# SwiGLU gates moved ahead of the second product, sixteen expert outputs summed in one PSUM bank, the token sort moved to the front of each mixture, and GpSimd in the GELU mixtures left with data movement alone

## The chip, the cores and the metric

One core of one Trainium2 chip runs the kernel. The metric is device time in microseconds (us) of one execution; the figure given is the median of three runs. The core's engines run side by side, each through its own list of instructions in order, and wait for each other on semaphores: PE (TensorE, matrix products), ACT (ScalarE), DVE (VectorE), POOL (GpSimd) and SP (SyncE, which here only issues DMAs).

## The reference

The network has four layers; each is a convolution-like mixer and then a mixture of experts over 8192 tokens of 64 channels, with a layer norm ahead of both. Layers 0 and 3 have a SwiGLU mixture of 16 experts of hidden size 128, layers 1 and 2 a GELU mixture of 8 experts of hidden size 256; each token uses the two experts with the largest router logits. Cut to the two mixtures:

```python
# SwiGLU, layers 0 and 3
h1 = jnp.einsum('bsd,edh->bseh', x, w1)
h2 = jnp.einsum('bsd,edh->bseh', x, w2)
hidden = jax.nn.silu(h1) * h2
expert_out = jnp.einsum('bseh,eho->bseo', hidden, w3)
return jnp.einsum('bseo,bse->bso', expert_out, dispatch)   # dispatch: two non-zero gates per token
# GELU, layers 1 and 2
for e in range(E):
    h = jax.nn.gelu(xf @ W1[e] + b1[e], approximate=False)
    out = out + w_dense[:, e:e + 1] * (h @ W2[e] + b2[e])
```

The third product is linear, so a SwiGLU gate may multiply the output of an expert or its hidden activations. In the GELU mixture the bias b2 stands between the product and the gate.

## The kernel before, in words

The tokens lie as 8 chunks of 512 columns, two halves of 64 channels stacked on the 128 partitions. In each mixture the first 6 chunks are *dense*: every expert is computed for every token and the gates (zeros among them) pick. A *step* is one expert on one chunk: 96 steps in SwiGLU, 48 in GELU; a *round* is two steps. The last 2 chunks (the pair SORTED) are *sorted*: DVE computes for each of their tokens a place in a list ordered by expert, POOL scatters the tokens to that list in DRAM (32 indirect DMAs, L757), the list is loaded (L792), worked off expert by expert in a *phase* on all engines (L824 to L924: 16 turns in SwiGLU, 12 in GELU, each with its own weights fetched by SP, L778 and L780), stored (L806), and POOL gathers two results for each token (32 indirect DMAs, L765), which are weighed (L942), merged on PE (L950) and added (L958). The phase interrupts the dense steps ahead of step `AFTER` (60 of 96, 30 of 48).

A SwiGLU step has three layers. PE forms the first (L1013, three products of split numbers); ACT applies Silu to both halves (L1167); PE forms the second, and DVE multiplies it in (L1187). Of an even step DVE multiplies both halves (128x1024), of an odd step one half; ACT copies the other half out of PSUM (L1157, `mx_kept`), and POOL multiplies it (L1268). PE forms the third layer into one of two small banks (L1099); DVE multiplies the result by the gates (L1194, `mx_gated`), and the product is added into `x` (L559): by POOL, or in the rounds in which POOL scatters or gathers (`by_vector`) by DVE. The gates are transposed by PE, written to DRAM (L539) and spread back over partitions by SP (L550, two DMAs of 128 KB a step, a ring of four slots).

A GELU step has two blocks of 128 hidden units: PE L1013, ACT Gelu L1401, PE L1350 into one of two small banks, DVE L1422 (bias and gate in one instruction), and the add (L559), again on POOL outside of the rounds with moves. POOL's list for GELU is: four conversions of tokens (L485), adds of steps 0 to 14, 32 scatters, 5 adds, 32 gathers, 5 adds.

The top-two choice is 17 small DVE instructions per pair of chunks (`choose`, L423 to L447; one Tanh on ACT, L455, lies ahead of the 13th), the sort 24 (`sort`, L691 to L746, with two count products on PE, L673). Before, both are handed out over the rounds of the first chunks (`between`, `behind`), the SORTED pair first. SP's one list serves all: spreads of gates, weights, the loads of sorted tokens (`load_at`, waiting for all scatters) and the stores. DVE's list, POOL's list and SP's list are written out by hand; nothing reorders them.

## Time and profile before

| | us |
|---|---|
| median of three runs (least, most) | 1908.18 (1907.76, 1908.95) |
| profiled execution | 1910.55 |
| its span in the trace | 1908.8 |
| busy PE, DVE, ACT, POOL in the span | 1630.5, 1163.1, 913.6, 780.2 |
| SwiGLU of layer 0, of layer 3 (first Silu to last add) | 350.7, 351.7 |
| GELU of layer 1, of layer 2 | 229.2, 232.3 |

Matmuls overlap in the records, so PE's busy time in a full stretch is near its length. "granted clock" is the share of TensorE's full 2.4 GHz that was granted; 0.50 is the lower of its two levels. The four mixtures take 1164 us of the 1908.8; the mixers and norms between them are not touched.

### The profile page before, as it was taken

How to read it: one execution, taken by the hardware profiler on the slowest of the kernel's cores; microseconds unless marked ns; L12 is line 12 of the kernel's file. 1: busy time of each engine (PE TensorE's matmuls, PEld its weight loads, DVE VectorE, ACT ScalarE, POOL GpSimd, SP SyncE). 2: the span in 40 equal slices, each digit the busy share in tenths (PEclk: the TensorE clock that was granted, in tenths of full speed). 3: DMA queues.
4: the chain of work that ended last, by engine and by line, in shares of the span. 5: the costliest groups of instructions: out<-in, count | busy, mean ns of one | idle time of the engine just before them, and what ended most of it. 6: DMA issues, size and time to landing. Idle time of an engine off the chain costs nothing. (4 is left out here: it accounts for less than half of the span.)

```text
span 1908.8 us, 32576 instructions
## 1 busy us (share of the span) xinstructions
PE 1630.5 (85%) x11943; PEld 928.0 (49%) x11943; DVE 1163.1 (61%) x1716; ACT 913.6 (48%) x1499; POOL 780.2 (41%) x711
## 2 busy tenths in 40 slices
PE   6878889789689979898978997999999678888787
PEld 3644444444244434444434445777777344444444
DVE  6678885387865512465631346665666478885386
ACT  2444444444236646435546544666666344434343
POOL 3316673176023623412360626333332036673275
PEclk8989999999799989999989998999999789999899
DMA  6012235242203443301253330000000012344233
GB/s 163 1 38 79 93 114 141 85 112 82 88 4 74 105 123 89 77 21 38 67 154 94 82 93 1 2 1 2 2 1 1 3 49 87 93 124 140 85 110 101
DMA packets 96922, 134.46 MB, mean 70 GB/s; under 512 B 31316, under 2 KB 48660, under 8 KB 96116
## 3 DMA queue, kind: packets, MB, share of 16 engines
q1 hardware_dynamic: 88564, 123.88, 22.9%
q0 software_dynamic: 8192, 8.40, 1.9%
q8 instruction: 99, 1.62, 0.4%
q14 instruction: 67, 0.55, 0.1%
HBM read 115.30 MB, written 16.91 MB: 69 GB/s over the span
## 5 line engine op out<-in xcount | busy, mean ns | idle before, releaser
L1013 PE MATMUL ps<-tokens_high,w_high 64*128 64x512 f32 x1152 | 259.8, 446 | 64.4 <-DVE mx_hidden L1187 56.3
L559 POOL TENSOR_TENSOR x<-x,mx_gated 128x512 f32<-128x512 f32 x144 | 188.7, 1311 | 285.7 <-DVE mx_gated L1422 218.5
L2458 DVE TENSOR_TENSOR c_near_weights<-c_near_hats 128x768 f32<-128x768 f32 x192 | 189.9, 1036 | 103.1 <-PE ps L2329 103.0
L1401 ACT ACTIVATE mx_hidden<-ps,w_bias 128x1024 f32<-128x1024 f32 x192 | 198.3, 1115 | 97.8 <-PE ps L1013 97.8
L1187 DVE TENSOR_TENSOR mx_hidden<-ps,mx_hidden 128x1024 f32<-128x1024 f32 x192 | 184.0, 958 | 88.3 <-PE ps L1013 86.9
L1013 PE MATMUL ps<-tokens_low,w_high 64*128 64x512 f32 x1152 | 234.0, 401 | 0.0
L1013 PE MATMUL ps<-tokens_high,w_low 64*128 64x512 f32 x1152 | 233.4, 400 | 0.0
L1268 POOL TENSOR_TENSOR mx_hidden<-mx_kept,mx_hidden 128x512 f32<-128x512 f32 x94 | 130.6, 1390 | 228.7 <-ACT mx_kept L1157 228.2
L1013 PEld LDWEIGHTS ps<-tokens_high,w_high 64*128 64x128 f32 x1152 | 111.8, 189 | 213.9 <-DVE mx_hidden L1187 133.3
L1350 PE MATMUL ps<-mx_hidden,w_second 128*64 128x512 f32 x768 | 184.4, 618 | 32.7 <-DVE mx_gated L1422 25.5
L1099 PE MATMUL ps<-mx_hidden,w_second 128*64 128x512 f32 x768 | 194.6, 624 | 9.4 <-DVE mx_gated L1194 6.6
L1422 DVE SCALAR_TENSOR_TENSOR mx_gated<-ps,w_bias,mx_gates 128x512 f32<-128x512 f32 x96 | 72.0, 750 | 213.8 <-PE ps L1350 146.6
L1167 ACT ACTIVATE mx_hidden<-ps 128x1024 f32<-128x1024 f32 x192 | 187.3, 1022 | 17.6 <-PE ps L1013 7.5
L1157 ACT COPY mx_kept<-ps 128x512 f32<-128x512 f32 x94 | 55.1, 587 | 276.1 <-PE ps L1013 270.0
L2407 ACT COPY c_near_matrix<-ps 128x512 f32<-128x512 f32 x288 | 149.0, 608 | 8.2 <-PE ps L2329 7.3
L757 POOL DMA_INDIRECT sorted_board<-mx_by_laid,mx_by_rows x128 | 128.8, 1006 | 42.5 <-issue 42.1
L2436 POOL TENSOR_TENSOR c_near_dist<-c_near_position,c_ints 128x288 f32<-128x288 f32 x64 | 65.1, 1017 | 193.8 <-DVE c_near_hats L2448 191.0
L765 POOL DMA_INDIRECT mx_by_tokens<-out_board,mx_by_rows x128 | 128.0, 1000 | 35.3 <-issue 33.4
L1194 DVE TENSOR_TENSOR mx_gated<-ps,mx_gates 128x512 f32<-128x512 f32 x192 | 127.9, 683 | 21.8 <-PE ps L1099 13.9
L2329 PE MATMUL ps<-identity,c_near_weights 128*128 128x128 f32 x1152 | 138.4, 277 | 0.0
L2358 PE MATMUL ps<-c_near_matrix,c_near_values 128*64 128x128 f32 (+1 forms) x1536 | 135.4, 329 | 0.0
L2329 PEld LDWEIGHTS ps<-identity,c_near_weights 128*128 128x128 f32 x1152 | 126.7, 142 | 11.4 <-issue 10.1
(275 smaller groups left out, 2416.1 us busy)
## 6 DMA issues: line engine op xcount, KB each, us to landing
mx_gates<-gate_board SPq DMA_DIRECT2D x576, 128.0 KB
mx_by_tokens<-sorted_board SPq DMA_DIRECT2D x14, 512.0 KB, 5.3
out_board<-mx_by_tokens SPq DMA_DIRECT2D x14, 512.0 KB, 2.8
w_first<-in_f_first SPq DMA_DIRECT2D x4, 1024.0 KB, 11.8
mx_by_first<-in_f_first_of SPq DMA_DIRECT2D x64, 64.0 KB
mx_by_second<-in_f_second_of SPq DMA_DIRECT2D x48, 65.0 KB
mx_by_first<-in_f_first_of SPq DMA_DIRECT2D x48, 64.2 KB
c_weight<-in_c_weight SPq DMA_DIRECT2D x1, 2304.0 KB
```

The source lines that it names most:

```text
L559: engine.tensor_tensor(place, place, gated, ALU.add).then_inc(self.s.added.semaphore, 1)
L1013: last = pe.matmul(out[h], weights[w][half(h), w_own], tokens[t][half(h), t_own], start=(p == 0), stop=(p == 2))
L1099: last = pe.matmul(out.bank("step", n)[half(h), :], w.second[:, e * C:(e + 1) * C], hidden[:, n % HIDDEN, h, :], start=True, stop=True)
L1167: act.activation(hidden[:, n % HIDDEN], first[:, n % FIRST], ACT.Silu).then_inc(s.act.semaphore, 1)
L1187: dve.tensor_tensor(own, second[:, 0:halves, :], own, ALU.mult).then_inc(s.hidden.semaphore, 1)
L1268: pool.tensor_tensor(own, kept[:, m // 2 % KEPT, :], own, ALU.mult).then_inc(s.other.semaphore, 1)
L1350: last = pe.matmul(out.bank("step", n)[half(h), :], w.second[:, (e * F + f) * C:(e * F + f + 1) * C], hidden[:, n % HIDDEN, f, h, :], star ...
L1401: act.activation(hidden[:, n % HIDDEN, f], first[:, (n * F + f) % BLOCKS], ACT.Gelu, bias=w.bias1[:, e * F + f:e * F + f + 1]).then_inc(s. ...
L2329: last = pe.transpose(turned[:, c % BANKS, at:at + P], weights[:, (HALVES * n + h) % SLOTS, t, q * P:(q + 1) * P], k.identity[:])
L2358: last = pe.matmul(acc[half(h), ty // (QTILES // 2), to:to + count * P], values[:, (v // G) % RING, g, h, t * C:(t + 1) * C], matrix[:, h, ...
L2407: act.copy(own, turned[:, c % BANKS, :].rearrange("p (h b c) -> p h b c", h=HALVES, c=P)).then_inc(s.matrix, 1)
L2458: dve.tensor_tensor(weights[:, u % SLOTS].rearrange("p t (r c) -> p t r c", c=W), spread(own[:, :, W:W + ROWS], 3, W), spread(own[:, :, 0: ...
```

## The change

SwiGLU:

- The gates multiply the hidden activations of a step after Silu and ahead of the second product: DVE those of half 0, POOL those of half 1 (both 128x512, both operands in SBUF). The spread gates now hold both halves on all partitions: one DMA of 512 KB a step in place of two of 128 KB.
- The third layers of a chunk's 16 experts accumulate in one PSUM bank (bank 6); DVE adds it into `x` once per chunk: 6 adds in place of 96. L1194 goes. The other small uses share bank 7.
- The multiply of the kept half moves from POOL (L1268) to DVE (`multiply_kept`).
- PE forms first layers one step further ahead.
- Scatters start at step 6 and gathers at step 50, two per round in place of three. The phase stands ahead of step 48 instead of 60.

Both mixtures:

- The choice of the SORTED pair (11 of its instructions) and the whole sort stand on DVE ahead of the first step; PE's count products stand in the first round.
- Loads and stores of the sorted tokens are issued by POOL and not by SP.

GELU:

- All 48 adds are on DVE. POOL's list is four conversions, 32 scatters, 3 loads, 3 stores, 32 gathers.
- The phase stands ahead of step 24 instead of 30. In it, the copies of columns and of outputs (with bias) move from ACT to DVE.

The core of the diff:

```diff
@@ class Gates, prefetch of step n
+        if self.of_hidden:
+            if n >= self.SLOTS:
+                self.s.gated_other.wait(sp, n - self.SLOTS + 1)
+            rows = self.board.rearrange("(h e) c -> e h c", h=HALVES)[e, :, chunk(i)]
+            sp.dma_start(self.spread[:, n % self.SLOTS, :, :], rows.partition_broadcast(P)).then_inc(
+                self.s.gate[n % self.SLOTS].semaphore, 16)
+            return
@@ class ByExpert
-    def load(self, sp):
+    def load(self, pool):
-    def store(self, sp, g):
-        self.s.turned.wait(sp, (g + 1) * (self.GROUP // 4))
-        sp.dma_start(self.group(self.out_board, g), self.own_group(g)).then_inc(self.s.stored.semaphore, 16)
+    def store(self, pool):
+        for g in range(self.m.slots // self.GROUP):
+            self.s.turned.wait(pool, (g + 1) * (self.GROUP // 4))
+            pool.dma_start(self.group(self.out_board, g), self.own_group(g)).then_inc(self.s.stored.semaphore, 16)
@@ mixture_swiglu, tensor
+            if e == 0 and i >= 1:
+                s.added.wait(pe, i)
             for h in range(HALVES):
-                last = pe.matmul(out.bank("step", n)[half(h), :], w.second[:, e * C:(e + 1) * C],
-                                 hidden[:, n % HIDDEN, h, :], start=True, stop=True)
+                last = pe.matmul(sums[half(h), :], w.second[:, e * C:(e + 1) * C],
+                                 hidden[:, n % HIDDEN, h, :], start=(e == 0), stop=(e == E - 1))
...
+            if n == 0:
+                gates.turn(pe, 0, small.bank("gates", 0))
+                for c in range(2):
+                    small.free(pe, "count", c)
+                    by.count_up(pe, c, small.bank("count", c))
             second_layer(n)
@@ mixture_swiglu, vector
+            s.gated.wait(dve, n + 1)
+            s.gated_other.wait(dve, n + 1)
             halves = HALVES if n % 2 == 0 or n == STEPS - 1 else 1
             own = hidden[:, n % HIDDEN, 0:halves, :]
             dve.tensor_tensor(own, second[:, 0:halves, :], own, ALU.mult).then_inc(s.hidden.semaphore, 1)
...
         def gate(n):
-            s.third.wait(dve, n + 1)
+            s.act.wait(dve, n + 1)
             gates.wait(dve, n)
...
+            own = hidden[:, n % HIDDEN, 0, :]
+            dve.tensor_tensor(own, own, gates.spread[:, n % gates.SLOTS, 0, :], ALU.mult).then_inc(s.gated.semaphore, 1)
...
         choose(0, 12, 17)
+        choose(SORTED, 0, 11)
+        sort(0, by.OPS)
+        gate(0)
         for n in range(0, STEPS, 2):
             if n >= 2 and n != AFTER:
                 multiply(n - 1)
-            between(n // 2)
+                multiply_kept(n - 1)
+            if n >= E + 2 and n % E == 2 and n - 2 != AFTER:
+                add(n // E - 1)
+            between(n)
+            gate(n + 1)
             multiply(n)
...
+            if n + 2 < STEPS:
+                gate(n + 2)
@@ mixture_swiglu, gpsimd
+            gate(n + 1)
+            if n == AFTER - 2:
+                by.store(pool)
+            if n + 2 < STEPS:
+                gate(n + 2)
...
+            if n == SCATTER_AT + 2 * (MOVES // EACH) + 2:
+                by.load(pool)
@@ mixture_gelu, vector
-            if by_vector(n):
-                gates.add(dve, n, gated[:, n % GATED, :])
+            gates.add(dve, n, gated[:, n % GATED, :])
...
         choose(0, 12, 17)
+        choose(SORTED, 0, 11)
+        sort(0, by.OPS)
@@ mixture_gelu, gpsimd
+        for i in range(2 * by.NT):
+            by.scatter(pool, i)
+        by.load(pool)
+        by.store(pool)
+        for i in range(2 * by.NT):
+            by.gather(pool, i)
```

In what follows each row is an instruction, a run of like ones with its count behind "x"; names are as in the text above, `gt_` those of the choice, `ln_square` and `mx_by_` those of the sort. DVE at the start of the first SwiGLU mixture before, from the last instruction of the first pair's choice (L447) on:

```order
L447 TENSOR_TENSOR gate<-gt_equal,gt_rank 128x256
L423 TENSOR_REDUCE gt_best<-gt_logits 128x16
L425 TENSOR_TENSOR gt_equal<-gt_logits,gt_best 128x256
L427 TENSOR_TENSOR gt_rank<-gt_equal,countdown 128x256
L1187 TENSOR_TENSOR mx_hidden<-ps,mx_hidden 128x1024
L1187 TENSOR_TENSOR mx_hidden<-ps,mx_hidden 128x512
```

The same place now (the first and the last rows of the 37 that stand between L444, which was L447, and the first multiply):

```order
L444 TENSOR_TENSOR gate<-gt_equal,gt_rank 128x256
L420 TENSOR_REDUCE gt_best<-gt_logits 128x16
L422 TENSOR_TENSOR gt_equal<-gt_logits,gt_best 128x256
...
L749 TENSOR_REDUCE mx_by_number<-mx_by_passed 1x32
L751 TENSOR_SCALAR mx_by_expert<-mx_by_number 1x32
L1222 TENSOR_TENSOR mx_hidden<-mx_hidden,mx_gates 128x512
L420 TENSOR_REDUCE gt_best<-gt_logits 128x16
L422 TENSOR_TENSOR gt_equal<-gt_logits,gt_best 128x256
L1222 TENSOR_TENSOR mx_hidden<-mx_hidden,mx_gates 128x512
L1211 TENSOR_TENSOR mx_hidden<-ps,mx_hidden 128x1024
```

Three instructions of the sorted pair stood ahead of the first multiply; now its whole choice but for the last part, the sort, two gates and two instructions of the next pair do. POOL in the rounds with scatters of SwiGLU before, a round to every two rows:

```order
L757 DMA sorted_board<-mx_by_laid,mx_by_rows 8192x64 x3
L1268 TENSOR_TENSOR mx_hidden<-mx_kept,mx_hidden 128x512
L757 DMA sorted_board<-mx_by_laid,mx_by_rows 8192x64 x3
L1268 TENSOR_TENSOR mx_hidden<-mx_kept,mx_hidden 128x512
L757 DMA sorted_board<-mx_by_laid,mx_by_rows 8192x64 x3
```

And now, with the loads behind the last scatters:

```order
L1287 TENSOR_TENSOR mx_hidden<-mx_hidden,mx_gates 128x512 x2
L762 DMA sorted_board<-mx_by_laid,mx_by_rows 8192x64 x2
L1287 TENSOR_TENSOR mx_hidden<-mx_hidden,mx_gates 128x512 x2
L762 DMA sorted_board<-mx_by_laid,mx_by_rows 8192x64 x2
L1287 TENSOR_TENSOR mx_hidden<-mx_hidden,mx_gates 128x512 x4
L797 DMA mx_by_tokens<-sorted_board 128x1024 x4
L1287 TENSOR_TENSOR mx_hidden<-mx_hidden,mx_gates 128x512 x5
L802 DMA out_board<-mx_by_tokens 128x1024 x4
```

A round held one tensor instruction and three moves on POOL; it holds two and two. POOL in a GELU mixture, whole, before:

```order
L485 TENSOR_TENSOR tokens_low<-xn,tokens_high 128x512 x4
L559 TENSOR_TENSOR x<-x,mx_gated 128x512 x15
L757 DMA sorted_board<-mx_by_laid,mx_by_rows 6144x64 x32
L559 TENSOR_TENSOR x<-x,mx_gated 128x512 x5
L765 DMA mx_by_tokens<-out_board,mx_by_rows 128x64 x32
L559 TENSOR_TENSOR x<-x,mx_gated 128x512 x5
```

And now:

```order
L482 TENSOR_TENSOR tokens_low<-xn,tokens_high 128x512 x4
L762 DMA sorted_board<-mx_by_laid,mx_by_rows 6144x64 x32
L797 DMA mx_by_tokens<-sorted_board 128x1024 x3
L802 DMA out_board<-mx_by_tokens 128x1024 x3
L770 DMA mx_by_tokens<-out_board,mx_by_rows 128x64 x32
```

The scatters no longer stand behind adds, and the loads stand right behind them on the same queue.

## Rows read from the trace of the kernel before

**Rows 1.** Table by stretch: length, busy us by engine, clock, DMA share, GB/s.
```profile
126.30:477.00 350.70, 298.23 (x1872) 157.39 (x1876) 255.34 (x358) 148.58 (x208) 196.80 (x163) 0.97 0.36 101
570.80:800.00 229.20, 203.10 (x1256) 100.09 (x1258) 90.48 (x165) 130.17 (x182) 99.54 (x92) 0.96 0.37 94
678.30:692.00 13.70, 5.29 (x22) 1.18 (x20) 1.49 (x2) 0.27 (x1) 3.50 (x3) 0.50 0.76 211
```
**Rows 2.** Waits of PE in layer 0's SwiGLU: total us, times, longest.
```profile
PE ps L1013 <- DVE mx_hidden L1187: 28.3, 30, 4.3
```
**Rows 3.** Timeline of ACT: start, us, instruction, [idle before <-releaser].
```profile
126.29 1.92 ACT L1167 ACTIVATE mx_hidden<-ps 128x1024 f32<-128x1024 f32 x2
...
233.81 1.94 ACT L1167 ACTIVATE mx_hidden<-ps 128x1024 f32<-128x1024 f32 x2
...
281.82 1.94 ACT L1167 ACTIVATE mx_hidden<-ps 128x1024 f32<-128x1024 f32 x2
293.92 1.94 ACT L1167 ACTIVATE mx_hidden<-ps 128x1024 f32<-128x1024 f32 x2
...
1865.78 0.59 ACT L1157 COPY mx_kept<-ps 128x512 f32<-128x512 f32 x1 [2.98 <-PE ps L1013]
1871.39 0.58 ACT L1157 COPY mx_kept<-ps 128x512 f32<-128x512 f32 x1 [2.96 <-PE ps L1013]
...
1884.11 0.59 ACT L1157 COPY mx_kept<-ps 128x512 f32<-128x512 f32 x1 [4.39 <-PE ps L1013]
1888.97 0.59 ACT L1157 COPY mx_kept<-ps 128x512 f32<-128x512 f32 x1 [2.21 <-PE ps L1013]
```
**Rows 4.** Timeline of POOL, two rounds with gathers.
```profile
1819.10 1.29 POOL L1268 TENSOR_TENSOR mx_hidden<-mx_kept,mx_hidden 128x512 f32<-128x512 f32 x1
...
1821.84 0.94 POOL L765 DMA_INDIRECT mx_by_tokens<-out_board,mx_by_rows  x1 [0.30 <-issue]
1823.09 0.94 POOL L765 DMA_INDIRECT mx_by_tokens<-out_board,mx_by_rows  x1 [0.30 <-issue]
1824.08 1.67 POOL L1268 TENSOR_TENSOR mx_hidden<-mx_kept,mx_hidden 128x512 f32<-128x512 f32 x1
```
**Rows 5.** Timeline of DVE: the same rounds, layer 0's early rounds, GELU's start, the end.
```profile
128.54 0.42 DVE L425 TENSOR_TENSOR gt_equal<-gt_logits,gt_best 128x256 f32<-128x256 f32 x1
129.00 0.42 DVE L427 TENSOR_TENSOR gt_rank<-gt_equal,countdown 128x256 f32<-128x256 f32 x1
129.34 1.22 DVE L1187 TENSOR_TENSOR mx_hidden<-ps,mx_hidden 128x1024 f32<-128x1024 f32 x1
...
134.64 1.39 DVE L433 SCALAR_TENSOR_TENSOR gt_logits<-gt_one_hot,gt_logits 128x256 f32<-128x256 f32 x1
...
582.81 0.29 DVE L427 TENSOR_TENSOR gt_rank<-gt_equal,countdown 128x128 f32<-128x128 f32 x1
...
1823.08 1.53 DVE L559 TENSOR_TENSOR x<-x,mx_gated 128x512 f32<-128x512 f32 x2
...
1902.10 0.69 DVE L559 TENSOR_TENSOR x<-x,mx_gated 128x512 f32<-128x512 f32 x1 [0.27 <-POOL x L559]
```
**Rows 6.** Waits of PE in layer 1's GELU.
```profile
PE ps L1350 <- DVE mx_gated L1422: 12.2, 5, 8.4
PE ps L514 <- DVE gate L447: 1.6, 1, 1.6
```
**Rows 7.** Timeline of PE around the phase's start in layer 1's GELU.
```profile
677.27 2.74 PE L1350 MATMUL ps<-mx_hidden,w_second 128*64 128x512 f32 x8 [2.41 <-DVE mx_gated L1422]
...
688.98 5.09 PE L1350 MATMUL ps<-mx_hidden,w_second 128*64 128x512 f32 x16 [8.41 <-DVE mx_gated L1422]
```
**Rows 8.** Timeline of SP's queue there.
```profile
680.62 1.29 SPq L792 DMA_DIRECT2D mx_by_tokens<-sorted_board  x3
```
**Rows 9.** Timeline of POOL: the last scatter there, and GELU's start.
```profile
572.41 4.99 POOL L485 TENSOR_TENSOR tokens_low<-xn,tokens_high 128x512 fp32r<-128x512 f32 x4 [11.47 <-DVE gate L447]
...
678.47 0.96 POOL L757 DMA_INDIRECT sorted_board<-mx_by_laid,mx_by_rows  x1 [0.30 <-issue]
```

More of the change, by code:

```diff
@@ L401, in __init__ @@
         self.pairs = k.mixtures * self.PAIRS
-        dense = m.dense // 2
-        order = [0] + list(range(dense, self.PAIRS)) + list(range(1, dense))
-        self.turn_of = {pair: i for i, pair in enumerate(order)}
     def done(self, pair):
@@ L587, in store @@
     def store(self, sp, i):
-        self.s.added.wait(sp, self.E * (i + 1))
+        self.s.added.wait(sp, self.adds * (i + 1))
         self.put(sp, i)
@@ L1015, in split_product, with out_order @@
     return last
-def out_order(steps, E, dense, turn_at, lay_at, count_at, after, merge_at):
-    order = [("gates", 0)]
-    for n in range(steps):
-        order.append(("step", n))
-        if n % E == turn_at and n // E + 1 < dense:
-            order.append(("gates", n // E + 1))
+def out_order(uses, dense, turn_at, lay_at, after, merge_at):
+    order = [("gates", 0), ("count", 0), ("count", 1)]
+    for n, own in enumerate(uses):
+        order += own
+        if n in turn_at:
+            order.append(("gates", turn_at.index(n) + 1))
         if n in lay_at:
             order.append(("lay", lay_at.index(n)))
-        if n == count_at:
-            order += [("count", 0), ("count", 1)]
         if n == after - 1:
@@ L1263, in _, with gate @@
     def _(pool):
-        def multiply(m):
-            s.act.wait(pool, m + 1)
-            s.kept.wait(pool, m // 2 + 1)
-            own = hidden[:, m % HIDDEN, 1, :]
-            pool.tensor_tensor(own, kept[:, m // 2 % KEPT, :], own, ALU.mult).then_inc(s.other.semaphore, 1)
-        pool.wait_ge(k.gt.gates, top_two.done(0))
-        for n in range(2, STEPS + 2, 2):
-            if n < STEPS:
-                multiply(n - 1)
-            if n % 4 == 2 and EARLY + n // 4 < DENSE:
-                token_low(k, pool, tokens, EARLY + n // 4)
-            for a in (n - 3, n - 2):
-                if a >= 0 and not by_vector(a):
-                    gates.add(pool, a, gated[:, a % GATED, :])
+        def gate(n):
+            s.act.wait(pool, n + 1)
+            gates.wait(pool, n)
+            own = hidden[:, n % HIDDEN, 1, :]
+            pool.tensor_tensor(own, own, gates.spread[:, n % gates.SLOTS, 1, :], ALU.mult).then_inc(
+                s.gated_other.semaphore, 1)
+        pool.wait_ge(k.gt.gates, top_two.done(0))
+        token_low(k, pool, tokens, EARLY)
+        gate(0)
+        for n in range(0, STEPS, 2):
+            gate(n + 1)
+            if n == AFTER - 2:
+                by.store(pool)
+            if n + 2 < STEPS:
+                gate(n + 2)
+            if 0 <= n - 8 < 2 * (DENSE - EARLY - 1):
+                token_low(k, pool, tokens, EARLY + 1 + (n - 8) // 2)
             for i in range(EACH):
@@ L1359, in second_layer @@
                 by.lay(pe, unit, out.bank("lay", unit))
-            if n == COUNT_AT:
-                for c in range(2):
-                    out.free(pe, "count", c)
-                    by.count_up(pe, c, out.bank("count", c))
             if n in MERGE_AT:
@@ L1373, in _ @@
                 gates.turn(pe, 0, out.bank("gates", 0))
+                for c in range(2):
+                    out.free(pe, "count", c)
+                    by.count_up(pe, c, out.bank("count", c))
             if n >= 2 and n != AFTER:
@@ L1481, in _ @@
             token_low(k, pool, tokens, i)
[L1482 to L1489 removed]
+        pool.wait_ge(k.gt.low, lows(k, DENSE - 1))
+        for i in range(2 * by.NT):
[4 more added lines that the diff above has]
+            by.gather(pool, i)
+        s.added.wait(pool, STEPS)
     @block.sync
```

332 lines of the change are left out of this document (150 added, 182 removed).

## The prediction

> **What bounds the kernel now.** I read the page first: PE is busy 85% of the span, the four mixtures take 1164 us of it, and only these change. Then the table by stretch for each mixture [rows 1]: in 350.70 us of SwiGLU PE is busy for 298.23, in 229.20 us of GELU for 203.10, so what can be won without touching a matmul is about 50 and 25 us a mixture, whoever is made faster. Then PE's waits show for whom it waits: in SwiGLU for DVE's multiply of the hidden activations [rows 2], 28.3 us in 30 pieces; in GELU for DVE's gate, 12.2 us in 5 pieces with one of 8.4 [rows 6].
>
> The starts of ACT's instructions give the length of a round of SwiGLU [rows 3]. A round in which POOL adds takes 4.86 us (1884.11 to 1888.97); ACT waits for PE in it, no round is shorter, and I take this as PE's own pace. A round in which DVE adds because POOL moves tokens takes 5.61 (1865.78 to 1871.39). The first 17 rounds, between which the choice and the sort are spread, take 233.81 - 126.29 = 107.5, against 17 x 4.86 = 82.6. One round takes 12.10 (281.82 to 293.92): SP stands in front of the load of sorted tokens there, and the gates behind it come late.
>
> Last I read single instructions of DVE and POOL side by side. POOL's multiply starts at 1824.08 while two adds of DVE (1823.08, 1.53 long, to 1824.61) run; it takes 1.67, against 1.29 at 1819.10, where no add of DVE runs [rows 4, 5]. On DVE the choice's instruction at 134.64 takes 1.39 while its neighbours of the same kind and size take 0.42 [rows 5]. Both have two operands in SBUF. So DVE and POOL hold each other up there, in both directions; the multiply that reads PSUM (1.22 at 129.34) shows no such spread.
>
> The Trainium skill says the same in "SBUF — State Buffer", section "Who interferes with whom": a DVE instruction with two SBUF inputs and a GpSimd instruction that reads SBUF exclude each other for a whole instruction. The trace agrees (1.67 for 1.29, 1.39 for 0.42). By that rule the change is a bad trade, since it turns DVE work that reads PSUM into work with two SBUF operands; this is my first rival, below, with its price from rows.
>
> **The change, part by part.** The sum is made against the profiled execution, 1910.55 us, which is 2.4 above the median of 1908.18; the difference is then taken off the median.
>
> *SwiGLU, what goes.* (a) The excess of the first 17 rounds: 107.5 - 82.6 = 24.9. (b) The excess of rounds with adds on DVE: 24 of them (steps 30 to 53 and 60 to 83), two already in (a), 22 x 0.75 = 16.5. (c) The load leaves SP's queue, so the round of 12.10 becomes an ordinary one: 6.5. (d) The last add waits for POOL's (0.27 at 1902.10 [rows 5]) and for a gate on DVE of 0.69 ahead of it: about 1. In the phase SP issues no stores between fetches: I take 1. Together 49.9.
>
> *SwiGLU, what comes.* (e) Ahead of the first multiply DVE has 11 instructions of the choice and 24 of the sort. The choice's pitch is 129.00 - 128.54 = 0.46 [rows 5]: 5.1. The sort at the same pitch is 11.0, and it goes through PE twice for the counts, some 1.5. POOL converts one chunk and multiplies its first gates meanwhile; each can hold DVE up as at 134.64, 1.39 - 0.42 = 0.97, so 2 for two of them. Together 19.6. Bounds: 16 (nothing held up, shorter instructions), 24 (every second instruction met by POOL). Nothing hides it: PE has two first layers in hand and then waits. PE at rest is granted the lower clock afterwards: where it rested 10.8 us around 680, the clock was 0.50 for 13.7 us [rows 1, 7]; I take 2 for it, from 0 to 7.
>
> (f) Rounds with moves: 16 for scatters, 16 for gathers. POOL has two multiplies (1.29) and two moves at a pitch of 1823.09 - 1821.84 = 1.25 [rows 4]: 5.08. DVE now has three instructions with two SBUF operands (two of 0.69 for gates or kept half, one more for the other gate), beside 1.22 + 0.69 that read PSUM: 3 x 0.69 + 1.91 = 4.0, so POOL is the longer list. It is held up by DVE as at 1824.08, 0.38. Once per round gives 5.46, so 32 x (5.46 - 4.86) = 19.2. Bounds: never, 32 x 0.22 = 7.0; both multiplies behind a whole instruction of 0.69 each, 5.08 + 1.38 = 6.46, 51.2. I take once, as the rows of a round with moves show one per round.
>
> (g) Choices of pairs 1 and 2 fall in 12 rounds, two instructions each, about one of them with two SBUF operands and so open to POOL: 0.97 x 8 = 7.8, from 0 to 12. (h) Six adds of the sum bank, 0.69 each and the wait of PE for the bank at each chunk: 3, from 0 to 6. (i) One gate DMA of 512 KB for 256 KB a step, and 16 rounds without moves: DVE's 4.0 and POOL's 2.6 lie beneath PE's 4.86, and DMA's mean share of 0.36 [rows 1] leaves room; 0, up to 5 if gates come late. (e) to (h): 19.6 + 2 + 19.2 + 7.8 + 3 = 51.6.
>
> So SwiGLU comes out at +1.7 a mixture, nought within what I can tell, and +3.4 for two. The adds removed (90 of 96) buy nothing by themselves, because rounds with adds on POOL already went at PE's pace.
>
> *GELU, what goes.* (j) PE stands 2.41 and 8.41 us ahead of the phase [rows 7]. SP shows why: the load of sorted tokens leaves it at 680.62, after the last scatter (678.47 + 0.96 [rows 9]), and the gates of the next steps stand behind that load in the same queue [rows 8]. With the load on POOL this goes: 10.8. What could be late next is the load itself, at 24 steps instead of 30: POOL has four conversions in 5 us and 32 scatters at the pitch of 1.25, 45 us together, and the scatters wait for a sort that ends some 14 us in, so they end near 60 us; step 24 of 48 stands at about half of the mixture's 229 less a share for the phase, some 80 to 100. 20 or more are left for the load. (k) The clock of 0.50 for 13.7 us, in which PE was busy for 5.29 [rows 1]: half of it, 2.6. (l) The turn of gates that waits for the choice, 1.6 [rows 6], as the choice is done earlier. (m) The rest of 12.2, where adds on POOL or DVE and choice meet: 1.4. (n) In merges, in the steps around the phase and in its turns small things, 3 together, bounds 0 and 6: moving columns and outputs from ACT to DVE can win only where PE waits for ACT, and none of PE's two large waits is for ACT [rows 6]. Sum 19.4.
>
> *GELU, what comes.* (o) DVE starts the sorted pair's choice when POOL starts its four conversions (572.41, 4.99 us for four [rows 9]). Choice of 11 at 0.29 + 0.04 [rows 5] is 3.6; each conversion holds DVE up once for about 1.0, so 7.6, then the sort's first instruction, and PE's counts come 6.9 later than PE would be free for them. PE stands for it, with 1.5 of lower clock behind: 8.4. Bounds 3 (conversions do not hold DVE up) and 14. The rest of the sort lies beside PE's next first layers and the trip of the first gates through DRAM. (p) All 48 adds on DVE: 0.69 each, 33 us at most on an engine that is busy for 90 of 229 [rows 1]: 0. Sum 8.4, so GELU gains 11.0 a mixture, 22.0 for two.
>
> Total: 3.4 - 22.0 = -18.6, 1908.2 - 18.6 = 1889.6. My bounds of (e) are as wide on the short side as on the long one, those of (f) lean to the long side, (n) and (m) to more gain. I forecast 1890.
>
> **The rivals.**
>
> *DVE and POOL lock each other out (slower).* Place: the 32 rounds with moves of each SwiGLU mixture. If both of POOL's multiplies wait for a whole instruction of DVE, and DVE's instructions wait likewise, a round takes 6.46 and not 5.46: 2 x 32 x 1.0 = +64 at the most; half of it, 5.96 per round, is the likelier form, +32: 1890 + 32 = 1922. It decides from 0.34 us per round on (22 us over 64 rounds, with which 1890 passes 1912). For it: 1.67 and 1.39 [rows 4, 5], and that each round holds five such instructions where it held three. Against it: POOL's moves, half of its round, show no change beside DVE's adds (0.94 throughout), and give DVE time for its own.
>
> *They hardly meet (faster).* PE runs further ahead, so DVE and POOL may fall into a pattern in which DVE's three instructions always lie beside POOL's moves. Then a round takes 5.08, (f) is 7.0 and (g) nought: -20 a mixture, 1890 - 40 = 1850. For it: two moves take 2.5, three DVE instructions 2.07. Against: DVE's order puts a PSUM multiply between them.
>
> *GELU's stall stays.* If scatters, now one string of 32 ahead of a load on the same queue, end late, or DVE's adds make gates late, (j) and (k) stay: 13.4 a mixture, 1890 + 26.8 = 1917; with half of it, 1903. Against: 20 us to spare.
>
> *The start costs more.* If the low clock holds after the opening, at 7 for 2 in SwiGLU and (o) at 14, with (e) at 24: 2 x (5 + 4.4 + 5.6) = +30, 1920. For it: a rest as long as this one is nowhere in these mixtures; against: (a) contains the same instructions, with the same locks.
>
> **How the numbers follow.** A measurement of this kernel can tell 0.2%, 3.8 us, from no change: faster is below 1904.4, slower above 1912. Chances: forecast 0.48 (1872 to 1904 alone), lock-out 0.19, hardly meet 0.14, GELU's stall 0.07, start 0.12. Faster: 0.47 of the forecast, 0.14, and 0.03 of partial cases of the others: 0.64. Slower: 0.15 of the lock-out, 0.03 and 0.07 of the last two: 0.25. Same is left with 0.11. The range leaves out a tenth on each side: the lower half of "hardly meet" and the upper third of lock-out and start: 1849 to 1928.
>
> **What would show it.** In GELU: no wait of PE for DVE's gate near the phase, loads on POOL that land before step 24, PE standing 6 to 8 us at the counts of the first round; the mixture at 218 us. In SwiGLU: the first multiply about 20 us later than before, rounds with moves at 5.3 to 5.6, rounds without at 4.9, no round above 8 after the start; the mixture at 350 +- 8. POOL's multiplies at 1.3 to 1.7. I am wrong if rounds with moves take 6 or more (first rival), or 5.1 (second); if PE waits for gates' DMAs at 512 KB; or if GELU does not fall by 8 or more a mixture.

## The result, and the profile after

The changed kernel takes 2000.26 us (median of four runs, 1998.91 to 2001.35) against 1907.97 for the kernel before: ratio 1.0487, 95% interval 1.0469 to 1.0505. I had forecast 1890 and a range up to 1928. It is slower by 92 us, and beyond every rival of mine.

Where the time stands is told first by the first and the last start of each mixture's activation. One line by source of before, then of the changed kernel: Gelu (duration in ns: least, median, most; then first and last start).

```profile
L1401 ACT ACTIVATE mx_hidden<-ps,w_bias x192: 1090/1115/1153, 570.8 to 1108.2; 128x1024 f32<-128x1024 f32 x192
```
```profile
L1420 ACT ACTIVATE mx_hidden<-ps,w_bias x192: 1096/1117/1156, 624.2 to 1144.1; 128x1024 f32<-128x1024 f32 x192
```

From the first Gelu of layer 1 to the last of layer 2 it was 537.4 us and is 519.9: the GELU part is faster. The first Gelu comes 53.4 us later. The first Silu comes 3.2 us later (129.5 for 126.29 [rows 3]), so some 50 us of that were lost in layer 0's SwiGLU. Of the 92 us, 92 - 53.4 + 17.5 = 56 are left for layer 3, so it loses about as much again. The table by stretch of the changed kernel, for layer 0's SwiGLU (answers to the first of [rows 1]) and for 25 us of its steady part:

```profile
129.50:529.00 399.50, 307.95 (x1862) 162.13 (x1862) 271.10 (x360) 151.82 (x206) 230.50 (x173) 0.91 0.70 152
425.00:450.00 25.00, 22.04 (x138) 11.13 (x136) 19.94 (x23) 11.58 (x13) 22.15 (x18) 1.00 0.92 173
```

The column before the last is DMA's mean busy share: 0.70 over the mixture where it was 0.36, and 0.92 in the steady part. In those 25 us the DMA engines are busy nearly all the time, and move 173 GB/s. The waits in this mixture (total us, times, longest) say who stands for it:

```profile
PE ps L1026 <- DVE mx_hidden L1211: 69.7, 40, 12.7
POOL mx_hidden L1287 <- DMA mx_gates<-gate_board: 51.8, 22, 8.2
DVE mx_hidden L1222 <- DMA mx_gates<-gate_board: 51.4, 27, 5.8
```

PE's wait for DVE's multiply is 69.7 us where it was 28.3 [rows 2], and DVE and POOL in their turn stand some 51 us each for gates that have not landed. In the kernel before no such wait was among the large ones of SwiGLU. The groups by form show the other cost: columns are busy us, mean ns of one, and idle time before.

```profile
L1287 POOL TENSOR_TENSOR mx_hidden<-mx_hidden,mx_gates 128x512 f32<-128x512 f32 x96 | 142.8, 1495 | 94.6 <-DMA mx_gates<-gate_board 51.8 <-ACT mx_hidden L1176 41.9
```
```profile
L1222 DVE TENSOR_TENSOR mx_hidden<-mx_hidden,mx_gates 128x512 f32<-128x512 f32 x96 | 92.8, 966 | 71.5 <-DMA mx_gates<-gate_board 51.4 <-ACT mx_hidden L1176 19.7
...
L1216 DVE TENSOR_TENSOR mx_hidden<-mx_kept,mx_hidden 128x512 f32<-128x512 f32 x47 | 42.4, 903 | 0.0
```

A multiply of 128x512 with two operands in SBUF takes 0.69 on DVE and 1.29 on POOL when nobody is in the way [rows 4, 5]. Here the means are 966, 903 and 1495 ns. POOL's moves take longer as well, though none has changed: the scatters 1.20 us on the mean (gathers 1.14) for 0.99 (1.02). The scatters of before, then of the changed kernel:

```profile
L757 POOL DMA_INDIRECT sorted_board<-mx_by_laid,mx_by_rows x32 | 31.8, 994 | 8.9 <-issue 8.6
```
```profile
L762 POOL DMA_INDIRECT sorted_board<-mx_by_laid,mx_by_rows x32 | 38.3, 1197 | 7.4 <-issue 6.5 <-DMA mx_gates<-gate_board 0.5
```

The start came nearly as forecast. DVE's timeline at the start of layer 0 (answers to the first three of [rows 5]):

```profile
131.79 1.27 DVE L422 TENSOR_TENSOR gt_equal<-gt_logits,gt_best 128x256 f32<-128x256 f32 x1
133.09 0.42 DVE L424 TENSOR_TENSOR gt_rank<-gt_equal,countdown 128x256 f32<-128x256 f32 x1
...
153.68 1.22 DVE L1211 TENSOR_TENSOR mx_hidden<-ps,mx_hidden 128x1024 f32<-128x1024 f32 x1
```

The first Silu stands at 129.5, so the first multiply comes 24.1 us behind it; before it came 129.34 - 126.29 = 3.1 behind it [rows 3, 5]. The sort in front costs 21.1 where I had 19.6; two gates and two instructions of the next pair's choice, which I had not priced, stand in it too. The table gives a granted clock of 0.51 for it:

```profile
133.00:160.00 27.00, 9.26 (x38) 5.53 (x36) 21.39 (x47) 4.01 (x5) 5.04 (x4) 0.51 0.56 121
```

In GELU the waits of PE are, in layer 1 (answers to [rows 6]):

```profile
PE ps L678 <- DVE ln_square L698: 6.3, 1, 6.3
PE ps L1370 <- DVE mx_gated L1442: 3.8, 2, 3.6
```

The wait of 12.2 for DVE's gate is down to 3.8, and the new wait for the counts of the sort is 6.3, where I had 6.9.

### The profile page after: what moved, and what is told of

Read it like the earlier page. It is cut to its first block and busy times, and to the rows that moved or that the text cites. A ratio compares the mean times of both kernels' runs of the same rounds, so it can differ in the third digit from the quotient of the medians.

```text
span 1999.6 us, 32592 instructions
## 1 busy us (share of the span) xinstructions
PE 1647.4 (82%) x11943; PEld 940.0 (47%) x11943; DVE 1232.4 (62%) x1822; ACT 907.4 (45%) x1451; POOL 790.8 (40%) x693
## 5 line engine op out<-in xcount | busy, mean ns | idle before, releaser
L1026 PE MATMUL ps<-tokens_high,w_high 64*128 64x512 f32 x1152 | 264.2, 454 | 163.6 <-DVE mx_hidden L1211 146.2
L1287 POOL TENSOR_TENSOR mx_hidden<-mx_hidden,mx_gates 128x512 f32<-128x512 f32 x192 | 285.2, 1493 | 194.1 <-DMA mx_gates<-gate_board 107.0
L1176 ACT ACTIVATE mx_hidden<-ps 128x1024 f32<-128x1024 f32 x192 | 196.4, 1025 | 228.6 <-PE ps L1109 210.2
L1222 DVE TENSOR_TENSOR mx_hidden<-mx_hidden,mx_gates 128x512 f32<-128x512 f32 x192 | 191.6, 998 | 145.3 <-DMA mx_gates<-gate_board 106.9
L1109 PE MATMUL ps<-mx_hidden,w_second 128*64 128x512 f32 x768 | 203.7, 652 | 5.5 <-DVE x L1227 4.0
L1370 PE MATMUL ps<-mx_hidden,w_second 128*64 128x512 f32 x768 | 181.6, 614 | 11.9 <-DVE mx_gated L1442 7.5
L762 POOL DMA_INDIRECT sorted_board<-mx_by_laid,mx_by_rows x128 | 142.6, 1114 | 62.5 <-issue 32.7
L770 POOL DMA_INDIRECT mx_by_tokens<-out_board,mx_by_rows x128 | 140.4, 1097 | 39.9 <-issue 31.3
L1026 PEld LDWEIGHTS ps<-tokens_high,w_low 64*128 64x128 f32 x1152 | 113.9, 193 | 27.2
```

The costliest lines, as they stand in the source:

```text
L762: pool.indirect_dma_start(out=self.sorted_board, in_=self.laid[:, t // HALVES, half(t % HALVES)], in_offset=None, out_offset=bass.Indirect ...
L1026: last = pe.matmul(out[h], weights[w][half(h), w_own], tokens[t][half(h), t_own], start=(p == 0), stop=(p == 2))
L1109: last = pe.matmul(sums[half(h), :], w.second[:, e * C:(e + 1) * C], hidden[:, n % HIDDEN, h, :], start=(e == 0), stop=(e == E - 1))
L1176: act.activation(hidden[:, n % HIDDEN], first[:, n % FIRST], ACT.Silu).then_inc(s.act.semaphore, 1)
L1222: dve.tensor_tensor(own, own, gates.spread[:, n % gates.SLOTS, 0, :], ALU.mult).then_inc(s.gated.semaphore, 1)
L1287: pool.tensor_tensor(own, own, gates.spread[:, n % gates.SLOTS, 1, :], ALU.mult).then_inc(s.gated_other.semaphore, 1)
```

## The experiments

Ratios are against the kernel before on the same chip, with 95% intervals; the changed kernel has 1.0487. The theories: *bandwidth* (a spread of 512 KB a step is more than the DMAs bring), *drain* (the four gate slots run empty once a chunk), *lock-out* (DVE and POOL hold each other up).

**1. GELU alone.** The kernel before, with the GELU mixture and the GELU phase of the change.

> The GELU half of the change alone; the SwiGLU mixtures as they were before. If the loss of 92 us lies in SwiGLU, as the starts of the stages say (+53 and +56 us a SwiGLU mixture, -18 to -20 for the two GELU mixtures together), this runs at 1886 to 1890 us. Rival: GELU's gain is bought with something that SwiGLU pays (loads on POOL, changed state of the DMA queues); then it stays at 1908 or above.

1886.27 us, ratio 0.9893 (0.9874 to 0.9912). The whole loss is SwiGLU's: 2000 - 1886 = 114 us for two mixtures.

**2. Earlier transposes.** In the changed kernel:

```diff
-    TURN_AT = [E * i + 9 for i in range(DENSE - 1)]
+    TURN_AT = [E * i + 5 for i in range(DENSE - 1)]
```

> The changed kernel, with the gates of the next chunk transposed behind step 5 of each chunk and not behind step 9; nothing else. Theory 'drain': SP stands in front of the post of the next chunk's gates until ACT has copied them, the four slots run empty meanwhile, five times a mixture at 5 to 6 us: 2000 - 50 = 1950 us. Theory 'bandwidth' alone (the spreads of 512 KB a step are limited to about 175 GB/s whenever they run): little, 1985 to 2000, since each round stays at 6.0 us. Theory 'lock-out' (DVE and POOL): no change, 2000.

1963.93 us, ratio 1.031 (1.0282 to 1.0339): 36 us come back, 3.6 for each of ten posts (five a mixture). What is undone is seen in the changed kernel's SP queue:

```profile
421.10 30.39 SPq L551 DMA_DIRECT2D mx_gates<-gate_board  x11
463.37 1.71 SPq L538 DMA_DIRECT2D gate_board<-xn  x4
465.19 2.81 SPq L551 DMA_DIRECT2D mx_gates<-gate_board  x4
```

Between 451.5 and 463.4 SP issues nothing: the next chunk's post (L538) waits for ACT's copy of its rows, which in the program stands behind the Silu of step 13 and comes at 463.09. DVE uses up the gates it has, and then stands 5.79 us for the next; its timeline, where the gate multiply starts at 470.85:

```profile
463.84 1.22 DVE L1211 TENSOR_TENSOR mx_hidden<-ps,mx_hidden 128x1024 f32<-128x1024 f32 x1
470.85 0.69 DVE L1222 TENSOR_TENSOR mx_hidden<-mx_hidden,mx_gates 128x512 f32<-128x512 f32 x1 [5.79 <-DMA mx_gates<-gate_board]
```

The place of the post was right as long as the gates met the third layer's output; now they meet Silu's, some steps earlier, and the post did not move with them. SP's waits for that copy were 45.6 us in 5 pieces in this mixture, and none is among its large waits with the early transposes. 'Drain' expected 50 us back and got 36; 'bandwidth' alone is out, and so is 'lock-out' alone, which expected no change.

**3. Half the bytes.** In the changed kernel one row of gates instead of two is spread:

```diff
-            rows = self.board.rearrange("(h e) c -> e h c", h=HALVES)[e, :, chunk(i)]
-            sp.dma_start(self.spread[:, n % self.SLOTS, :, :], rows.partition_broadcast(P)).then_inc(
+            sp.dma_start(self.spread[:, n % self.SLOTS, 0, :], self.board[e, chunk(i)].partition_broadcast(P)).then_inc(
```

> The changed kernel, with one DMA of 256 KB a step in place of 512 KB: both halves read the gates of half 0, so the second half's outputs are gated wrongly; no instruction of any engine is changed in kind or number. Theory 'bandwidth': the ordinary rounds fall from 6.0-6.2 to 5.2-5.5, some 40 rounds a mixture, 2000 - 60 = 1940 us, the drains stay. Theory 'drain' alone: 1990 to 2000. Theory 'lock-out': 2000.

1954.38 us, ratio 1.0243 (1.022 to 1.0265): 46 back, where 'bandwidth' expected 60. POOL multiplies by the same row as DVE here, so the gates of half 1 are left out.

**4. Both edits**, those of runs 2 and 3.

> Both edits together (gates of the next chunk transposed behind step 5; one DMA of 256 KB a step, the second half gated wrongly). If bandwidth and drain are all that the prediction missed, its own sum returns: 1890 us, 1880 to 1905. If the lock-out of DVE and POOL is a third part, it stays above 1915, with rounds with moves of 5.8 or more.

1925.2 us, ratio 1.0099 (1.0068 to 1.0129): 75 back, nearly the sum of the two, and 35 short of my own sum. The clause on a third part holds: a rest is left. The gates' DMAs have little part in it: in layer 0 DVE waits for them no longer, and POOL 7.4 us where it was 51.8. POOL's group of this run:

```profile
L1286 POOL TENSOR_TENSOR mx_hidden<-mx_hidden,mx_gates 128x512 f32<-128x512 f32 x96 | 136.8, 1436 | 66.0 <-ACT mx_hidden L1175 57.9 <-DMA mx_gates<-gate_board 7.4
```

**5. POOL's gate cut short**, to 8 of 512 columns, on top of both:

```diff
-            pool.tensor_tensor(own, own, gates.spread[:, n % gates.SLOTS, 0, :], ALU.mult).then_inc(
+            pool.tensor_tensor(own[:, 0:8], own[:, 0:8], gates.spread[:, n % gates.SLOTS, 0, 0:8], ALU.mult).then_inc(
```

> Both edits of the run before (early transposes, one DMA of 256 KB a step) and POOL's gate multiplies 8 of 512 columns only (the rest of half 1 stays ungated), so that POOL holds SBUF for a fraction of the 1.3 us, with the same instructions and waits. Theory 'lock-out': the rest that is left (1925 against my sum of 1890, rounds that alternate between 4.85 and 6.6 also where POOL moves nothing) goes: rounds of 4.9 to 5.2, 1925 - 50 = 1875 us, 1865 to 1885. Rival 'ring': Silu of step n waits for the third layer of step n-4, and the gate now stands between Silu and the multiply, so the loop itself is too long: 1915 to 1925, rounds as before.

1839.14 us, ratio 0.9658 (0.9639 to 0.9676): 86 us, where 'lock-out' expected 50; 'ring', as it was put (rounds as before), is out. POOL's gate stands in the ring's loop too, and a shorter one shortens that loop; runs 6 and 10 come back to it. DVE's own instructions became short, though not one of them was changed. The groups of the run with both edits:

```profile
L1221 DVE TENSOR_TENSOR mx_hidden<-mx_hidden,mx_gates 128x512 f32<-128x512 f32 x96 | 109.7, 1143 | 26.2 <-ACT mx_hidden L1175 26.2
```

and of the run with POOL cut short:

```profile
L1221 DVE TENSOR_TENSOR mx_hidden<-mx_hidden,mx_gates 128x512 f32<-128x512 f32 x96 | 66.3, 691 | 34.2 <-ACT mx_hidden L1175 33.9
```

1143 ns to 691, 43 us of DVE's time in one mixture, and it stands in the chain that PE waits for. Shorter POOL work also shortens POOL's list in rounds with moves; so the 86 is the price of POOL's multiply as a whole, not of the lock alone. Run 10 comes back to this.

**6. A ring of six** slots for the hidden activations, on top of both edits (the spread gates keep one half only, which makes the room; that part of the edit is not shown):

```diff
-    FIRST, HIDDEN, KEPT = 2, 4, 2
+    FIRST, HIDDEN, KEPT = 2, 6, 2
```

> Both edits (early transposes, one DMA of 256 KB a step, second half gated wrongly) and the hidden activations in a ring of six slots and not four (the gates' unused half of SBUF pays for it), so Silu of step n waits for the third layer of step n-6. Theory 'ring': rounds fall to 5.0 to 5.4, 1880 to 1895. Theory 'lock-out': POOL and DVE still hold each other up, and nothing is gained: 1915 to 1925.

1958.83 us, ratio 1.0293 (1.0265 to 1.0321): 33 slower than without, which neither theory expected. DVE's gate multiplies take 1357 ns on the mean, for 1143. The timelines show what happens, DVE and POOL of this run:

```profile
245.19 3.21 DVE L1221 TENSOR_TENSOR mx_hidden<-mx_hidden,mx_gates 128x512 f32<-128x512 f32 x1
```
```profile
245.34 2.50 POOL L1286 TENSOR_TENSOR mx_hidden<-mx_hidden,mx_gates 128x512 f32<-128x512 f32 x2
```

With two more slots ACT gives POOL both activations of a round at once (1.94 for two, with no wait between), POOL runs two multiplies back to back, and DVE's instruction of 0.69 stands for both: 3.21. More room made the collisions longer.

**7. Wide rows.** Early transposes and the full 512 KB, but the board laid out so that both halves' rows of an expert lie side by side:

```diff
+            self.wide = self.board.rearrange("r c -> (r c)").rearrange("(e i h c) -> e i h c", e=E, i=CHUNKS, h=HALVES)
...
+            row = self.wide[e, i, :, :].rearrange("h c -> (h c)")
+            sp.dma_start(self.spread[:, n % self.SLOTS, :, :].rearrange("p h c -> p (h c)"), row.partition_broadcast(P)).then_inc(
```

> The changed kernel with early transposes and the full 512 KB a step, but the gate board laid out so that the two rows of an expert lie side by side and a partition's 4 KB come from one stretch (eight small posts a chunk instead of four). Beside the run with early transposes alone (1964): if the limit of about 175 GB/s is one of packets, half as many packets free it and the time falls towards the run with 256 KB (1925 to 1940); if it is one of bytes read from one place, 1960 to 1975.

1928.33 us, ratio 1.0135 (1.0115 to 1.0156), within noise of the run with half the bytes (run 4), and inside what was expected if packets are the limit. So the bytes are not. The same 25 us as above, in this run:

```profile
425.00:450.00 25.00, 22.09 (x146) 12.07 (x146) 21.44 (x23) 11.90 (x15) 23.10 (x18) 1.00 0.60 188
```

It moves 188 GB/s at a share of 0.60, where the changed kernel moved 173 at 0.92. SP's queue in these 25 us (packets, MB, share of the 16 DMA engines' time), of before, the changed kernel, run 4 and run 7:

```profile
q1 hardware_dynamic: 1280, 2.10, 28.3%
```
```profile
q1 hardware_dynamic: 2097, 4.04, 84.5%
```
```profile
q1 hardware_dynamic: 1481, 2.42, 32.7%
```
```profile
q1 hardware_dynamic: 1439, 4.37, 53.1%
```

The share of 16 x 25 us, by the packets, is the time of one: 88 ns before, 161 in the changed kernel, 88 in run 4, and 148 in run 7, where twice as many bytes travel in about as many packets as in run 4. So the changed kernel did not only send more packets; each took nearly twice as long. Run 7 changed two things at once, the number of packets and where the rows lie in DRAM, and no run tells which of them does it.

**8. GELU, and SwiGLU's load on POOL.** Run 1, with the load of sorted tokens in the old SwiGLU issued by POOL ahead of step 56.

> The GELU half of the change, and in the otherwise old SwiGLU mixtures only the load of the sorted tokens moved from SP to POOL, ahead of step 56. The old SwiGLU has one round of 12.1 us (layer 0) where SP stands in front of that load, and two of 8.7 and 9.0 (layer 3), against 4.9 to 5.6: 6.5 us a mixture, so 1886 - 12 = 1874 us. Rival: POOL stands in front of the load instead, its multiply comes late, and the round stays long: 1884 to 1890.

1900.82 us, ratio 0.9983 (0.9968 to 0.9999), 14 us worse than run 1 and outside of both expectations. ACT's timeline still has the long round (answers to [rows 3]), and POOL's shows the load late:

```profile
280.95 1.94 ACT L1223 ACTIVATE mx_hidden<-ps 128x1024 f32<-128x1024 f32 x2
...
292.49 1.94 ACT L1223 ACTIVATE mx_hidden<-ps 128x1024 f32<-128x1024 f32 x2
```
```profile
308.93 2.22 POOL L800 DMA_DIRECT2D mx_by_tokens<-sorted_board  x4
```

292.49 - 280.95 = 11.54 for 12.10: the load was not the cause. The trace of before says so already: the load left SP at 298.92 there, when the long round had ended (293.92 [rows 3]). It leaves POOL at 308.93 here, just ahead of the phase, which then waits: from the last Silu ahead of the phase to the first behind it are 66.7 us (309.19 to 375.85), for 60.1 in run 1 (308.39 to 368.47).

**9. Fetches apart.** Run 1, with SP's six early fetches of expert weights in the old SwiGLU three or four steps apart instead of two.

> The GELU half of the change alone (1886 us), and in the otherwise old SwiGLU mixtures the six early fetches of expert weights by SP at steps 36, 39, 43, 47, 51, 55 in place of 38, 40, 42, 44, 46, 48. The round of 12.1 us did not go when the load of sorted tokens left SP; the trace shows DVE waiting 3.7 us for gates behind a run of fetches instead, then PE at the lower clock. Theory 'fetches': 6 us a mixture come back, 1874 to 1880. Rival: the gates are late for another reason, 1884 to 1890.

1882.76 us, ratio 0.9879 (0.9856 to 0.9901). The round that took 12.10 takes 6.15 in its profile, but the next takes 8.66 (starts at 283.46, 289.61 and 298.27); of 12 expected some 3 came, inside the intervals of the two, and the time lies between the two expectations. So the run of fetches is in that round; how much it is worth is open.

**10. All gates on DVE**, on run 7. DVE multiplies both halves in one instruction, POOL's multiply goes; nothing is left out.

```diff
-            own = hidden[:, n % HIDDEN, 0, :]
-            dve.tensor_tensor(own, own, gates.spread[:, n % gates.SLOTS, 0, :], ALU.mult).then_inc(s.gated.semaphore, 1)
+            own = hidden[:, n % HIDDEN, :, :]
+            dve.tensor_tensor(own, own, gates.spread[:, n % gates.SLOTS, :, :], ALU.mult).then_inc(s.gated.semaphore, 1)
```

> The changed kernel with early transposes and the gate board in wide rows (1928 us as a run before), and now DVE multiplies both halves by their gates in one instruction of 128x1024; POOL multiplies nothing in the dense steps of SwiGLU, it only moves tokens. Nothing of the computation is left out. Theory 'lock-out': DVE has more work (two of 1.2 for two of 0.69, 5.1 us a round and so the bound), yet the time falls, since no instruction of DVE or POOL waits for the other any more: 2 x 48 x 0.3 above the run with POOL's gate cut short (1839), 1865 to 1885 us. Rival 'DVE is full': if DVE was the bound already and POOL a relief, it rises: 1935 to 1960.

1879.6 us, ratio 0.9872 (0.9847 to 0.9897). DVE got 2 x (1.23 - 0.69) = 1.1 us more work a round, POOL lost 2.6, and the kernel became 49 us faster, inside what 'lock-out' expected. Its groups and ACT's starts:

```profile
L1232 DVE TENSOR_TENSOR mx_hidden<-mx_hidden,mx_gates 128x1024 f32<-128x1024 f32 x96 | 118.2, 1232 | 14.4 <-ACT mx_hidden L1187 9.6 <-DMA mx_gates<-gate_board 1.4 <-issue 0.3
```
```profile
394.69 1.02 ACT L1187 ACTIVATE mx_hidden<-ps 128x1024 f32<-128x1024 f32 x1 [1.44 <-PE ps L1120]
...
399.93 1.02 ACT L1187 ACTIVATE mx_hidden<-ps 128x1024 f32<-128x1024 f32 x1 [1.51 <-PE ps L1120]
```

One instruction for both halves takes 1232 ns, no more than its size asks for (the like one out of PSUM takes 1.22), and a round without moves is 399.93 - 394.69 = 5.24 us. POOL's last gather of layer 0 stands well ahead of it:

```profile
383.62 1.12 POOL L781 DMA_INDIRECT mx_by_tokens<-out_board,mx_by_rows  x1 [0.30 <-issue]
```

The edit does two things: DVE and POOL no longer meet over multiplies, and POOL's list gets shorter in rounds with moves. To see the meeting with little of the second, take the round of run 7 behind its last gather, ACT's starts and what DVE and POOL do in it:

```profile
452.80 1.02 ACT L1189 ACTIVATE mx_hidden<-ps 128x1024 f32<-128x1024 f32 x1 [1.97 <-PE ps L1122]
...
458.85 1.02 ACT L1189 ACTIVATE mx_hidden<-ps 128x1024 f32<-128x1024 f32 x1 [2.62 <-PE ps L1122]
```
```profile
453.86 2.26 DVE L1235 TENSOR_TENSOR mx_hidden<-mx_hidden,mx_gates 128x512 f32<-128x512 f32 x1 [0.64 <-ACT mx_hidden L1189]
```
```profile
453.01 2.54 POOL L1300 TENSOR_TENSOR mx_hidden<-mx_hidden,mx_gates 128x512 f32<-128x512 f32 x2
```

DVE's 0.69 becomes 2.26 beside POOL's two multiplies, and the round takes 6.05. The same two steps in run 10:

```profile
431.29 1.02 ACT L1187 ACTIVATE mx_hidden<-ps 128x1024 f32<-128x1024 f32 x1 [1.67 <-PE ps L1120]
...
436.47 1.02 ACT L1187 ACTIVATE mx_hidden<-ps 128x1024 f32<-128x1024 f32 x1 [1.44 <-PE ps L1120]
```

They take 5.18. So the meeting of the two engines has a price of its own, though DVE has more work in run 10. How the 49 us part between the meetings and POOL's shorter list is open.

This version is faster than the kernel before by 27 us. Of these, 21 are GELU's (run 1): beside run 1 it is 6.7 us faster, and the intervals of the two overlap. So even in this form the SwiGLU half of the change is not shown to win.

**11. GELU's load back on SP**, at step 20, in run 1.

> The GELU half of the change alone (1886 us), with the load of the sorted tokens back on SP, at step 20 of 24. The scatters still stand early and in one string on POOL. My prediction put GELU's stall down to SP standing in front of that load. If that is so because the scatters were late, they are done by now, and nothing changes: 1884 to 1889. If the place of the load in SP's queue is itself the cause, the two stalls of about 11 us return: 1905 to 1912.

1892.61 us, ratio 0.9925 (0.9899 to 0.995). By its time, between the two expectations, this is inconclusive, but PE's long wait did not return. PE's waits in layer 1's GELU:

```profile
PE ps L681 <- DVE ln_square L701: 5.5, 1, 5.5
PE ps L1401 <- DVE mx_gated L1473: 3.1, 2, 2.8
```

3.1 us, and 12.2 before [rows 6]. Yet a part of the stall is there in this profile: right behind the load DVE stands 3.93 us for its gates, and from the Gelus ahead of the phase to those behind it are 707.69 - 651.08 = 56.6 us, for 47.1 in run 1 (654.19 to 701.29) and 61.7 before (670.86 to 732.54). DVE, then ACT, of this run:

```profile
660.54 0.75 DVE L1473 SCALAR_TENSOR_TENSOR mx_gated<-ps,w_bias,mx_gates 128x512 f32<-128x512 f32 x1 [3.93 <-DMA mx_gates<-gate_board]
```
```profile
651.08 4.13 ACT L1451 ACTIVATE mx_hidden<-ps,w_bias 128x1024 f32<-128x1024 f32 x4 [0.61 <-PE ps L1053]
...
707.69 5.14 ACT L1451 ACTIVATE mx_hidden<-ps,w_bias 128x1024 f32<-128x1024 f32 x5 [5.70 <-PE ps L1053]
```

So the late scatters made PE's long wait, and in this profile the place of the load in SP's queue keeps a price of its own. The profiled execution took 1901.59 us, the longest of six. By the medians the load costs 6 us, and the intervals of the two runs overlap, so how much it is worth is open.

**12. No kept half**, on run 10: DVE multiplies both halves of every step out of PSUM (two of 1.22), and ACT's copy and DVE's multiply of the copy go.

> The run with all gates on DVE (1880 us), and DVE multiplies both halves of every step straight out of PSUM (128x1024, two of 1.22); ACT's copy of the kept half and DVE's multiply of it (0.69 + 0.69 for 1.22) go. Nothing of the computation is left out. DVE's list per round falls from 5.06 to 4.90, near PE's 4.86. Theory 'DVE's list is the bound now': 0.15 to 0.3 us a round, 1852 to 1866. Rival 'PE waits for the bank': the second layer's bank is held 0.53 longer in every odd step, and PE loses what DVE wins: 1876 to 1895.

1902.45 us, ratio 0.9991 (0.9974 to 1.0009): 23 slower than run 10: the direction is the rival's, the size beyond its 1876 to 1895. Two of ACT's starts are a round of 406.80 - 401.24 = 5.56 us, for 399.93 - 394.69 = 5.24 in run 10:

```profile
401.24 1.02 ACT L1177 ACTIVATE mx_hidden<-ps 128x1024 f32<-128x1024 f32 x1 [2.04 <-PE ps L1116]
403.62 1.02 ACT L1177 ACTIVATE mx_hidden<-ps 128x1024 f32<-128x1024 f32 x1 [1.36 <-PE ps L1037]
406.80 1.02 ACT L1177 ACTIVATE mx_hidden<-ps 128x1024 f32<-128x1024 f32 x1 [2.16 <-PE ps L1116]
```

ACT waits for PE ahead of each. PE in its turn waits for a bank until DVE has read it, as the rival says, but not for long. PE's waits between 390 and 450 us, of this run and of run 10 (total us, times, longest):

```profile
PE ps L1037 <- DVE mx_hidden L1207: 4.3, 10, 0.6
```
```profile
PE ps L1037 <- DVE mx_hidden L1221: 3.1, 9, 1.1
```

The 1.2 us between them are about 0.1 a round, of the 0.32; what makes the rest is open.

## Why the prediction was wrong, point by point

**GELU was right.** -22.0 was forecast for two mixtures, 1907.24 to 1886.27 is -21. The stall ahead of the phase went, as (j) said. Run 11 bears out both halves of (j): with early scatters alone PE's long wait is gone, and with the load still on SP some 9 us more pass across the phase of the one execution that was profiled. The start of (o) was 6.9 and measured 6.3.

**The step that failed first is (i)**, "0, up to 5 if gates come late". I set 512 KB against a mean share of 0.36, as if DMA time were to be had at any moment and a packet cost the same however many stand together. What failed is the second half of that. At the price before, twice the packets would have filled 0.57 of the DMA engines' time from SP's queue; they filled 0.845, since a packet took 161 ns for 88 (run 7). At the 173 GB/s of that stretch the 1.05 MB of a round take 6.1 us, for PE's 4.86. No byte rate was the limit: [rows 1] have 211 GB/s for a stretch of before, and run 7 moves the same bytes at 188 with 0.40 of the engines' time to spare. It cost 36 us (run 7 against run 2) to 46 (run 3 alone). My own sign, "if PE waits for gates' DMAs at 512 KB", came true by way of DVE, which waited for them and was waited for by PE.

**The drain was not in the sum at all**, and no rival named it. I priced what the moved instructions cost. I did not ask when their gates are posted: the use of the gates moved some steps ahead, and the place of the post in SP's queue did not. It cost 36 us (run 2).

**(f) and (g) had the right mechanism at too small a size.** Of the sum, 54 us for the two mixtures stood for POOL's longer list and for DVE and POOL holding each other up; run 5 takes 86 away. POOL's side came out about as I had it: 1436 for 1290 ns (run 4), twice a round, is 0.29 for my 0.38. What (f) put at nothing is DVE's side: 1143 for 691 ns on its gate multiplies, twice a round, is 0.9 us, and it stands in the chain that PE waits for. Nor does it fall in rounds with moves alone, as the round of run 7 shows (2.26 for 0.69). My first rival named this and bounded it by one DVE instruction per POOL multiply; the longer wait is DVE's, through one POOL multiply or two (0.69 becomes 3.21 in run 6). What I held against it, that POOL's moves show no change, did not hold either: 1.20 and 1.14 in the changed kernel.

The Trainium skill had it in "SBUF — State Buffer", section "Who interferes with whom": the other engine fully blocks. The trace agrees (2.50 for two POOL multiplies inside DVE's 3.21), and I gave it a chance of 0.19 where all the change's new multiplies fall under it. In that pair DVE's record starts 0.15 us ahead of POOL's, and yet DVE is the one that waits: the starts of records don't tell which of the two goes first.

**(e) was right**: 21.1 for 19.6. **(a)** too, as far as run 5 shows it: there, with POOL cut short, the 17 rounds from the first Silu to step 34 (127.53 to 234.09) take 106.6, against 107.5 before, so the sort in front costs what it had cost between the rounds. **(c) had a wrong cause.** The load did not make the round of 12.10 (run 8). In the trace of before DVE stands 3.70 us in it, ahead of a multiply by gates:

```profile
283.96 0.69 DVE L1194 TENSOR_TENSOR mx_gated<-ps,mx_gates 128x512 f32<-128x512 f32 x1 [3.70 <-issue]
```

The row names no releaser. That these are gates behind SP's fetches is argued from SP's queue, and run 9 bears it out for that round (6.15). I had seen two things close together in SP's queue and had not read what stood directly ahead of the wait. (b), (d), (h) and the 2 us for PE's lower clock were not measured by themselves.

The sum put right: 1889.6 + 36 (drain) + 36 (packets) + 86 - 54 (lock-out) = 1993.6; 2000.3 was measured, and 7 us are not accounted for. That the rest of my sum comes out is in part luck, since (c)'s 6.5 had a wrong cause. The parts were taken away one behind the other, so their sizes hold in that order; run 3 alone shows that another order moves some 10 us between the first two.

## What to carry to other kernels

When a change moves the use of data to an earlier point of a pipeline, walk back along the chain that feeds it (here transpose, copy, post, spread) and ask at which step each link is issued: whatever stays where it was becomes the new wait. Neither a mean DMA share nor the byte rate of another stretch is a price for more DMA: here a packet took nearly twice as long when twice as many stood in the queue, so try the DMA by itself, and try twice the bytes in packets of twice the size, which cost little here. And where work on operands in SBUF is split between DVE and POOL, try the whole of it on DVE first: here that was faster.

## What the runs showed that I had not expected

- 2 KB packets of one row spread to 128 partitions moved 173 GB/s at a busy share of 0.92; packets of 4 KB moved 188 GB/s at 0.60 in the same place, and the kernel was 36 us faster than with 2 KB packets (run 7 for run 2).
- A DVE instruction of 0.69 us stood for two POOL multiplies in a row (3.21 us), and with the deeper ring, which lets POOL work in pairs, the kernel was 33 us slower.
- Giving DVE 1.1 us more work a round and POOL none made the kernel 49 us faster.
- The best form of the SwiGLU half (1879.6 us) is not clear of the GELU half alone (1886.27 us).
